# A new order of the work items in a two-layer transformer kernel: Q's and K's stacks apart, the cuts of the maxima further ahead of their transposes, the held residual behind the up matrices

## The chip, the cores and the metric

One core of one Trainium2 chip. The metric is the device time of one launch in microseconds (us). Before the change it was 1240.19 us, the median of 3 runs.

## What is computed

Eight batches of 512 tokens with 256 channels go through two layers. Layer 0 is a conditioned transformer block with a causal mask and an MLP, layer 1 an attention without mask between two conditioned normalizations. Cut to what matters:

```python
def layer0(x, condition):                    # x: (8, 512, 256) float32, condition: (8, 256)
    mod = silu(condition) @ Wada + bada      # (8, 1536)
    sh_a, sc_a, gt_a, sh_m, sc_m, gt_m = split(mod, 6, axis=1)
    xm = layernorm(x, g1, be1) * (1 + sc_a) + sh_a
    q, k, v = heads(xm @ Wqkv)               # 16 heads of 16 channels
    s = where(causal, q @ k.T / 4, -inf)
    x = x + gt_a * (merge(softmax(s) @ v) @ Wproj + bproj)
    xm = layernorm(x, g2, be2) * (1 + sc_m) + sh_m
    return x + gt_m * (gelu(xm @ W1 + b1) @ W2 + b2)      # W1: 256 -> 1024

def layer1(hidden, w):
    h = sln(hidden, w)                       # gamma(w) * layernorm + beta(w)
    q, k, v = heads(h @ Wqkv.T + bqkv)
    out = merge(softmax(q @ k.T) / 16 @ v) @ Wp.T + bp
    h1 = out + hidden
    return sln(h1, w) + h1
```

## The kernel before

**Order.** All the work is a sequence of items, written out by hand in three lists of tokens. HEAD is run once (for the passes -1, 0 and 1), RING once for each of the passes 2 to 6, TAIL once (7, 8 and 9); pass i has layer 0's batch i beside layer 1's batch i-1. `one_list` (L206) walks a list and calls the same function `work` for each engine, so TensorE (PE), VectorE (DVE), ScalarE (ACT), GpSimd (POOL) and the DMA queue of SyncE (SP) each get their own part of every item, all in the order of the list. An engine never overtakes within its own queue. Semaphore counts, banks and buffers follow from the order by counters (`ADDS`, L100 on).

**Items of attention.** There are 16 heads, 4 query tiles, and 16 steps (4 groups of heads by 4 key tiles) for each layer and batch.
- `s`, a scan: scores of one head and query tile, to find each row's maximum. PE makes them in a PSUM bank (L972, and L975 for the mask in layer 0), DVE takes the maximum (L759, 128, 256, 384 or 512 wide in layer 0, always 512 in layer 1). Scans share four banks with all dense items.
- `nm..`: POOL cuts the negated maxima of eight heads ("a" or "b"; of four heads with `_0` to `_3`) in three parts, four instructions (L575 to L581). `max..`: PE transposes them (L1117), ACT copies (L684) and its own queue moves them under the queries (L686). An attention step of those heads waits for that DMA.
- `a` and `p`: three heads, then the fourth, of one step: scores transposed on PE (L953) and the exponentials on ACT (L621). In layer 0 POOL masks the diagonal (L541).
- `o`: the products of two steps with V (L942). `t`: ACT copies a group's output to OE (L636).
- `pack` (SP, L439 and L441, five DMAs), `recip` (SP, L447 and L452, the reciprocals to DRAM and spread back), `scale` (DVE, L907), or `fold` and `merge` in the first and last batch: the division by the sums.

**Other items.** `stat` and `norm` (DVE, L768 and L808) normalize, `turn` (PE L1052, ACT L651) transposes and modulates, `q`, `k` (L1064) and `v` multiply; q and k are cut into three bf16 parts in PART by ACT (L666), DVE (L834 to L842) and POOL. `stackq` and `stackk` (SP, L416, 12 DMAs each in two halves of the heads) copy these parts into QS and KS, where the scans and scores read them:

```python
for part in range(3):
    wait(sp, (high_act, cut_low, cut_low)[part], ready[part])
    for r in range(CUTS):
        if parts[r] == part:
            sp.dma_start((QS, KS)[side][n][r:CUT_ROWS:CUTS, heads, :],
                         PART[rows, side, part, :, :]).then_inc(stack_dma[n][half], 16)
```

At `stackq` SP waits until ACT has done the exponentials of all scores ahead of it in the list, then issues Q's first half (6 DMAs); at `stackk` it issues K's first half, Q's second and K's second (18). A scan that begins a half of the heads waits on PE for that half of Q and K. `proj` (L1037 with WP, DVE L871 and L875) adds the attention to the residual. `up_0` to `up_7` (PE L1088, ACT L671 with Gelu, another table of ACT than that of Exp) and `down_0` to `down_3` (L1037 with W) are the MLP. `row0`, `row1`, `keep0` are SP's loads of the row vectors and the next batch (L461, L467, L474); with row0 goes an addition on POOL (L587). `hold1` is an addition on POOL (L596) of layer 1's bias to the residual that is kept for proj1. `gain1` and `close1` end layer 1. `mods` is 24 products of 128 x 128 weights with 8 columns, in pairs (48 matmuls, L918), which make the modulation; its first eight pairs are made before the lists. `rows` (PE L1017) turns the row vectors and, on SP, issues the loads of the later weights.

**Places.** In a pass, the items between k1 and turn_a hold most scans of layer 1, which are all 512 wide; behind turn_a come layer 0's q, k, v, projection and MLP.

Of the kernel before, what the change touches and what calls it, by code (L numbers as in the profile page):

```python
# [58 lines left out]
HEAD = """
    stat_a norm_a turn_a q0 stackq0 k0 stackk0 mods rows s v0 s s s s s s s s s s s s s s s s s s s s s s s s s  # L60
    s s s s s s s nm0_0 s s max0_0 s s s s s s s s a s s s s row0 s p a s nm0_1 s keep0 p s s s a s max0_1 p o a
    p a s o s nm0_2 s p a s s s p s s a stat_a t max0_2 s p s o a p a nm0_3 p o a t norm_a p a max0_3 p turn_a o
    fold0_0 a p a o t p a p fold0_1 a p o a p q0 o fold0_2 t fold0_3 merge0 proj0 stackq0 k0 norm_m v0 stackk0
    turn_m up_0 s up_1 s s s s up_2 s s up_3 s s s s s up_4 s s s s s up_5 s s s s s up_6 s s s s up_7 s s s s s
    s down_0 s nm0a down_1 max0a down_2 down_3 s a s s s p s a p norm_1 s s o s s s a s s row0 p turn_1 s a s s
    s s keep0 s s stat_a s p q1 k1 stackq1 s norm_a o v1 s a stackk1 s s t s p s a s s s s s p turn_a s a s s
    nm0b p max0b s s a s s s o s p s s a s s o s p s a s p s s s t a s o s p s a s p s a s s p s s o s s t a s p
    a s s s nm1a s p s o s a s p s max1a s o t pack0 s recip0 v0 s s a q0 p s a s s p scale0 s s s a stackq0 o p
    proj0 a s s norm_m p k0 a s s o p turn_m a s s s up_0 s t up_1 up_2 up_3 stackk0 s s p up_4 up_5 s a s s s o
    p s s nm1b hold1 s a s s p s s up_6 s s up_7 o s max1b down_0 a down_1 p down_2 s a s s t p down_3 a o s p s  # L70
    a s s p s s s a s p s s s s s a s s o s p s s t a s s norm_1 nm0a s s o p s turn_1 s a s s s max0a q1 p s k1
    s""".split()
# [8 lines left out]
TAIL = """
    stackq1 o t a s s s p s s pack1 a s p s a s s p stackk1 a s s o p s a s s recip1 s s o s s p s s s t s a s
    nm0b s row1 p a s p s s max0b s a s s o s s p s a s s o s s s p s a s p s a s s t s s p a o p s s a s s o t
    s s row0 s p s a s s p s nm1a scale1 s a o p s a max1a s p proj1 o s t a s v1 pack0 recip0 gain1 p s a s p a
    p s s a s o p scale0 s s o close1 proj0 a p s s norm_m s s a p a s hold1 turn_m s s s s up_0 s up_1 up_2
    up_3 up_4 s s up_5 up_6 s s up_7 s s down_0 s down_1 t down_2 s s p nm1b down_3 max1b a norm_1 o p o turn_1
    a q1 t k1 p a p stackq1 stackk1 a p a o s s p s s a s s s o s t s p s s a s p s s s a s nm1_0 p s s o row1 s
    max1_0 s s a s s s s s p o s s a s p s s a s s p v1 s t nm1_1 a s p s max1_1 s s a s o s pack1 s p s s a s p
    s recip1 o s a s s p s nm1_2 s a s p t s s max1_2 s s s a s s o s p s a s keep0 o t s p s s a p fold1_0
    nm1_3 a o p max1_3 scale1 a proj1 p gain1 a p o t a close1 p a p o row1 a p fold1_1 o fold1_2 hold1 t  # L90
    fold1_3 merge1 proj1 gain1 close1""".split()
# [1084 lines left out]
```

How the kernel before makes its waits and increments, by code:

```python
def wait(eng, sem, value):  # L150
    if value > 0:
        eng.wait_ge(sem, value)
# [239 lines left out]
        @block.sync  # L392
        def _(sp):
            sp.dma_start(CT[:], cond_t).then_inc(cond_load, 16)
            by_row = wada.rearrange("(k p) n -> p k n", p=P)
            sp.dma_start(WADA[:, :, 0:2 * D], by_row[:, :, 0:2 * D]).then_inc(ada_load, 16)
            sp.dma_start(XIN[:], x[0].rearrange("(t p) d -> p t d", p=P)).then_inc(x_dma, 16)
            sp.dma_start(WQKV[0][:], wqkv0.rearrange("(k p) n -> p k n", p=P)).then_inc(qkv_load[0], 16)
            sp.dma_start(WADA[:, :, 2 * D:6 * D], by_row[:, :, 2 * D:6 * D]).then_inc(mod_load, 16)
            sp.dma_start(WGB, wgb1.rearrange("(k p) n -> p k n", p=P)).then_inc(mod_load, 16)
            sp.wait_ge(ones_pool, 1)
            for n in range(2):
                sp.dma_start(KS[n][CUT_ROWS:ALL_ROWS, :, :], ONES).then_inc(ones_load, 16)
# [13 lines left out]
            def work(at, kind, what, b):  # L419
                if kind != "chunk":
                    return
                if what == "rows":
                    sp.wait_ge(set_dve, ROWS_READY)
                    sp.dma_start(rows_dram, ROWS.rearrange("p (r d) -> p r d", d=D)).then_inc(rows_out, 16)
                    sp.dma_start(WP[0][:], wproj0.rearrange("(k p) n -> p k n", p=P)).then_inc(proj_load[0], 16)
                    sp.dma_start(W1[:], w1.rearrange("(k p) n -> p k n", p=P)).then_inc(up_load, 16)
# [75 lines left out]
            run_passes(work)
            sp.wait_ge(store_dma, 16 * (B + 1))
```

## Time and profile before

| | |
|---|---|
| runs | 1240.56, 1240.19, 1234.33 us, median 1240.19 |
| profiled execution, its own time | 1239.17 us |
| its span | 1237.4 us |
| mean granted clock of PE | 0.986 |
| busy: PE, DVE, ACT, POOL | 94%, 69%, 55%, 23% |
| HID to down: PE, mean of one 128x256 matmul (L1037, W) | 380 ns |
| maximum, mean over all widths (L759) | 583 ns x1024 |
| exponential, mean over all widths (L621) | 524 ns x1024 |

Times in the profile are microseconds from the start of the span, unless ns is written. PE's matmuls overlap in their pipeline and their ends are modelled, so its busy share says less than the chain of work that ended last: that chain is followed back from the last instruction, at each step to what released it or to the instruction before it on its engine, and its shares say who set the end. The waits list an engine's idle time by what ended it.

### The profile page before, as it was taken

To read this page: it belongs to the slowest core of one execution; us is meant where nothing else is said; L and a number is where in the kernel's file an instruction comes from. 1 tells how busy PE (TensorE), PEld (TensorE's weight loads), DVE (VectorE), ACT (ScalarE), POOL (GpSimd) and SP (SyncE) were. 2 spreads that over 40 slices of the span, in tenths; PEclk is the share of its full clock that TensorE was granted. 3 is DMA by queue.
4 is the path that set the end of the run, shared out by engine and by line. 5 is a ranking of instruction groups with operands and counts; after the bars stand their busy time and mean duration, and the time that the engine had idled before them with its cause. 6 is when DMAs were issued, how large, how long until landed. Compare 5 with 4: busy or idle time off the path is not lost.

```text
span 1237.4 us, 18599 instructions
## 1 busy us (share of the span) xinstructions
PE 1164.9 (94%) x6604; PEld 591.7 (48%) x6604; DVE 849.1 (69%) x1779; ACT 676.6 (55%) x1346; POOL 279.7 (23%) x378
## 2 busy tenths in 40 slices
PE   7888999999999998999899999999989999999995
PEld 5434644464444644555345644546445553445332
DVE  4835498637886579836887379855888368764775
ACT  1173245656557465565656466565645656553673
POOL 1133032311432024301233013320233002310003
PEclk9799999999999999999999999999999999999999
DMA  4603031302432042500623024410425005200311
GB/s 166 206 2 103 3 124 33 107 14 72 111 93 65 18 113 71 139 2 18 164 44 115 2 80 104 105 54 18 118 66 139 1 2 148 55 17 32 86 33 43
DMA packets 59190, 89.35 MB, mean 72 GB/s; under 512 B 12914, under 2 KB 23762, under 8 KB 59098
## 3 DMA queue, kind: packets, MB, share of 16 engines
q1 hardware_dynamic: 58078, 87.35, 25.4%
q8 instruction: 53, 0.87, 0.3%
q10 hardware_dynamic: 1020, 0.81, 0.2%
q14 instruction: 39, 0.32, 0.1%
HBM read 24.41 MB, written 4.70 MB: 24 GB/s over the span
## 4 chain that ended last, share of the span: by engine, by line
PE 63%; DVE 19%; ACT 5%; SPq 5%; DMA 3%; issue 3%; POOL 1%; ACTq 0%; DVEq 0%; POOLq 0%
PE X L1037 15%; DVE MX L759 10%; PE OP L942 10%; PE X L1064 9%; PE X L1088 9%; PE SC L953 8%; PE X L972 8%; SPq L416 4%; ACT E L621 3%; DMA OC<-OE 2%; DVE STAT L768 2%; DVE XN L808 2%; DVE XR L875 1%; DVE TMP L871 1%; PE X L1052 1%
## 5 line engine op out<-in xcount | busy, mean ns | idle before, releaser
L759 DVE TENSOR_REDUCE MX<-X 128x1 f32<-128x512 f32 (+3 forms) x1024 | 533.2, 583 | 178.4 <-PE X L975 95.4
L621 ACT ACTIVATE E<-SC 128x512 f32<-128x512 f32 (+3 forms) x1024 | 459.0, 524 | 325.8 <-PE SC L953 258.6
L972 PE MATMUL X<-KS,QS 96*128 96x512 bf16 (+3 forms) x1024 | 296.5, 346 | 11.6 <-DVE MX L759 7.5
L953 PE MATMUL SC<-QS,KS 99*128 99x512 bf16 (+3 forms) x1024 | 276.1, 342 | 19.6 <-ACT E L621 12.6
L942 PE MATMUL OP<-E,V 128*32 128x512 f32 (+3 forms) x2048 | 208.2, 524 | 5.2 <-ACT OE L636 5.0
L953 PEld LDWEIGHTS SC<-QS,KS 99*128 99x128 bf16 x1024 | 93.7, 97 | 168.3 <-ACT E L621 105.9
L972 PEld LDWEIGHTS X<-KS,QS 96*128 96x128 bf16 x1024 | 97.4, 98 | 160.2 <-DVE MX L759 52.9
L541 POOL TENSOR_SCALAR_AFFINE_SELECT E<-E 128x512 f32<-128x512 f32 x128 | 87.0, 683 | 249.1 <-ACT E L621 249.1
L1088 PE MATMUL X<-XT,W 128*128 128x512 f32 x256 | 119.1, 598 | 1.2 <-ACT XT L651 1.2
L1064 PE MATMUL X<-XT,WQKV 128*128 128x512 f32 x256 | 118.2, 607 | 1.4 <-ACT XT L651 1.4
L1037 PE MATMUL X<-W,HID 128*128 128x256 f32 x512 | 115.3, 380 | 0.3 <-ACT HID L671 0.3
L975 PE MATMUL X<-CAUSAL,ID 128*128 128x128 bf16 x512 | 105.8, 223 | 0.0
L942 PEld LDWEIGHTS OP<-E,V 128*32 128x32 f32 x2048 | 53.9, 110 | 108.2 <-issue 79.3
L1037 PEld LDWEIGHTS X<-W,HID 128*128 128x128 f32 x512 | 96.3, 190 | 14.0 <-ACT HID L671 0.8
L555 POOL TENSOR_TENSOR RSTD<-VE,HALF 128x4 f32<-128x4 f32 x32 | 32.9, 1029 | 275.2 <-DVE VE L773 274.4
L671 ACT ACTIVATE HID<-X,VF 128x512 f32<-128x512 f32 x64 | 43.3, 687 | 58.7 <-PE X L1088 58.4
L1064 PEld LDWEIGHTS X<-XT,WQKV 128*128 128x128 f32 x256 | 48.7, 194 | 53.5 <-issue 49.3
L871 DVE TENSOR_TENSOR TMP<-X,ROW 128x512 f32<-128x512 f32 x32 | 22.0, 687 | 74.9 <-PE X L1037 74.9
L575 POOL TENSOR_SCALAR NMP<-MX 128x32 bf16<-128x32 f32 (+1 forms) x36 | 8.7, 242 | 281.6 <-DVE MX L759 256.8
L1088 PEld LDWEIGHTS X<-XT,W 128*128 128x128 f32 x256 | 46.4, 190 | 45.1 <-issue 41.5
L975 PEld LDWEIGHTS X<-CAUSAL,ID 128*128 128x128 bf16 x512 | 51.3, 100 | 22.7 <-issue 8.8
L1037 PE MATMUL X<-WP,OC 128*128 128x256 f32 x256 | 58.7, 382 | 1.6 <-issue 0.8
(92 smaller groups left out, 922.9 us busy)
## 6 DMA issues: line engine op xcount, KB each, us to landing
QS<-PART SPq DMA_DIRECT2D x192, 128.0 KB, 2.4
KS<-PART SPq DMA_DIRECT2D x192, 128.0 KB, 2.5
OC<-OE SPq DMA_DIRECT2D x56, 128.0 KB, 3.8
RB<-recip_sums SPq DMA_DIRECT2D x56, 128.0 KB, 2.6
XIN<-in_x SPq DMA_DIRECT2D x8, 512.0 KB, 4.9
ROW<-row_vectors SPq DMA_DIRECT2D x8, 512.0 KB, 3.7
out<-OUT SPq DMA_DIRECT2D x7, 512.0 KB, 3.2
W<-in_w SPq DMA_DIRECT2D x2, 1024.0 KB, 7.3
```

What stands on the lines that cost most here:

```text
L416: sp.dma_start((QS, KS)[side][n][r:CUT_ROWS:CUTS, heads, :], PART[rows, side, part, :, :]).then_inc(stack_dma[n][half], 16)
L541: g.affine_select(out=block, in_=block, compare_op=ALU.is_ge, fill=zero, base=0, pattern=[[0, 4], [1, P]], channel_multiplier=-1)\
L621: a.activation(E[:, at["tick"].index() % 3, j, lo:T], SC[(at["head"].index() + j) % 3][:, lo:T], ACT.Exp, scale=HD ** -0.5 if layer == 0 e ...
L671: a.activation(HID[:, ht, :], bank(0)[:], ACT.Gelu, bias=B1[:, ht:ht + 1])\
L759: v.reduce_max(MX[:, qt, h:h + 1], X[at["bank"].index() % BANKS][:, 0:w], AX.X, negate=True)\
L942: ins = t_.matmul(OP[32 * j:32 * j + 32, lo:T], V[layer][:, kt, h * VW:h * VW + 32], E[:, (at["step"].index() + n) % 3, j, lo:T], start=kt ...
L953: t_.matmul(SC[(at["head"].index() + j) % 3][:, lo:T], KS[stacks(layer, b)][0:ALL_ROWS, h, kt * P:kt * P + P], QS[stacks(layer, b)][0:ALL_ ...
L972: ins = t_.matmul(bank[:, 0:w], QS[stacks(layer, b)][0:CUT_ROWS, h, qt * P:qt * P + P], KS[stacks(layer, b)][0:CUT_ROWS, h, 0:w], start=Tr ...
L975: ins = t_.matmul(bank[:, qt * P:w], ID16[:], CAUSAL[:], start=False, stop=True)
L1037: ins = t_.matmul(psum[:, t % 2 * D:t % 2 * D + D], rows[:, kt, t * P:t * P + P], weights(kt), start=kt == 0, stop=kt == depth - 1)
L1064: ins = t_.matmul(psum[:], WQKV[n][:, kt, lo:lo + P], XT[:, kt, :], start=kt == 0, stop=kt == KT - 1)
L1088: ins = t_.matmul(psum[:], W1[:, kt, ht * P:ht * P + P], XT[:, kt, :], start=kt == 0, stop=kt == KT - 1)
```

## The change

Only the three lists are changed. Each holds the same tokens as before, in another order; no instruction is added, removed or changed in shape. In the middle passes stackq0 moves from behind q0 to behind turn_m, away from k0, and hold1 from behind turn_m to behind up_7; nm1a moves ahead of v1 and apart from max1a, nm0b and max0b further apart, and pack1 ahead of stackk1. In HEAD, mods moves from behind the first stacks to ahead of the first turn_a, and the first q0 of batch 1 behind merge0. In TAIL the order of the first stretch stays about the same and the folds move. The scans and steps between are spread anew. The middle list and the first lines of HEAD:

```diff
@@ -57,38 +57,39 @@
 EARLY = 9
 HEAD = """
-    stat_a norm_a turn_a q0 stackq0 k0 stackk0 mods rows s v0 s s s s s s s s s s s s s s s s s s s s s s s s s
-    s s s s s s s nm0_0 s s max0_0 s s s s s s s s a s s s s row0 s p a s nm0_1 s keep0 p s s s a s max0_1 p o a
-    p a s o s nm0_2 s p a s s s p s s a stat_a t max0_2 s p s o a p a nm0_3 p o a t norm_a p a max0_3 p turn_a o
-    fold0_0 a p a o t p a p fold0_1 a p o a p q0 o fold0_2 t fold0_3 merge0 proj0 stackq0 k0 norm_m v0 stackk0
-    turn_m up_0 s up_1 s s s s up_2 s s up_3 s s s s s up_4 s s s s s up_5 s s s s s up_6 s s s s up_7 s s s s s
...
+    stat_a norm_a mods turn_a q0 stackq0 k0 stackk0 rows v0 s s s s s s s s s s s s s s s s s s s s nm0_0 s
+    s s max0_0 s s s s s s s s s nm0_1 a s s s s p s s a s p s s s a s p max0_1 s s s a row0 s keep0 s o
+    nm0_2 p a s s s p s s max0_2 o s s t a s s s s p s a p o a s s s p a o t s nm0_3 p a fold0_0 p max0_3 a
+    o p a p a fold0_1 p stat_a norm_a o t a p fold0_2 a p o a p o t turn_a fold0_3 merge0 q0 stackq0 proj0
+    k0 norm_m v0 turn_m up_0 up_1 up_2 stackk0 s s s s s s up_3 s s up_4 s s s s s s s s up_5 s s s s s s
+    up_6 s s up_7 s s s s s s s s nm0a down_0 down_1 max0a s down_2 s s s down_3 a s s s s p a p s s s a s
...
 RING = """
-    row0 s stackq1 a s p o a stackk1 s s t s s s p s s pack1 s a s o s s s p s s a s s s p s s a s s s p o s
-    nm0b s s recip1 a max0b s s s p s a s p s s t s a s o s s p s a s scale1 s p o row1 a s t s p proj1 a s s p
-    o s a p a p s s s o s t a keep0 s p s s s a s gain1 p o close1 a nm1a stat_a max1a s v1 p norm_a a o t s
-    pack0 p s turn_a s a s recip0 s s q0 p s s s a o stackq0 p s s a s scale0 k0 s s p proj0 a s s norm_m p v0 a
-    o s s p turn_m hold1 s s a s s t s p up_0 up_1 s o s a s s s up_2 s s up_3 stackk0 p s s nm1b up_4 up_5 s
-    up_6 max1b s o s s up_7 t s s a s s down_0 s p down_1 s a s s p down_2 down_3 a o s p s s a s s p s s s s a
-    s norm_1 s o s p s s s a s s s s s p turn_1 a s nm0a s s t max0a s p q1 a s s o p s k1 s""".split()
+    stackq1 o s t s s s a s row0 p s row1 s s s a s s pack1 s stackk1 p s s a s p s s a s s recip1 s o s s
+    s s p a s s s nm0b p s s keep0 o t a s s s p a s max0b s s p s s s o s a s s p a s s p o scale1 a s s s
+    p proj1 t o a s s s s p a p a s s p o t s s a s nm1a s p gain1 close1 stat_a v1 a max1a o s norm_a p a
+    p a s s p o t pack0 turn_a s a s s s recip0 q0 p s s s a o p s s s a s s scale0 p k0 s s a proj0 p v0
+    norm_m a o p s s turn_m s a stackq0 t s s s up_0 up_1 s s p s o s a s s s p s o t stackk0 s s s up_2
+    nm1b up_3 up_4 up_5 max1b s up_6 up_7 s s s a s s s hold1 down_0 down_1 p s s s a down_2 down_3 p s s a
+    o p s a s s s p s s s a s s p norm_1 o s s s s a s s s p t turn_1 s a o s s p s s a s nm0a s s s p q1
+    max0a s k1""".split()
 TAIL = """
-    stackq1 o t a s s s p s s pack1 a s p s a s s p stackk1 a s s o p s a s s recip1 s s o s s p s s s t s a s
-    nm0b s row1 p a s p s s max0b s a s s o s s p s a s s o s s s p s a s p s a s s t s s p a o p s s a s s o t
-    s s row0 s p s a s s p s nm1a scale1 s a o p s a max1a s p proj1 o s t a s v1 pack0 recip0 gain1 p s a s p a
...
+    stackq1 s a o t p s s a s row1 s p s s s o s s s s a s s s p s s pack1 a s s p a s stackk1 s s s s nm0b
+    p s o t s a s s s recip1 p a max0b s s p s o s a s s p s a s s p o s t a s p s s s a s s p o s s a s s
+    p a s s p o s t a s s p s nm1a s s row0 a scale1 s p o a s s p proj1 gain1 o t pack0 recip0 s max1a v1
+    a p s s s a p row1 s s s s a s s o s scale0 p a p s close1 proj0 a s s norm_m o p a p s s turn_m a s s
...
```

## Rows read from the trace of the kernel before

**Rows 1.** The page, part 4: the chain that ended last, by engine
```profile
PE 63%; DVE 19%; ACT 5%; SPq 5%; DMA 3%; issue 3%; POOL 1%; ACTq 0%; DVEq 0%; POOLq 0%
```

**Rows 2.** That chain in order of time: start, us, engine and operation
```profile
558.17 6.92 PE X L1037 x32
...
580.03 3.43 PE X L1064 x8
584.51 1.85 PE OP L942 x16
...
642.04 0.65 PE X L972 x3
```

**Rows 3.** Windows: stretch, length, busy PE, PEld, DVE, ACT, POOL, clock, DMA share, GB/s
```profile
733.62:783.70 50.08, 46.02 (x340) 22.19 (x339) 45.98 (x100) 29.30 (x76) 18.01 (x27) 1.00 0.41 111
783.70:877.00 93.30, 93.01 (x472) 49.09 (x471) 58.26 (x120) 55.99 (x93) 17.24 (x17) 1.00 0.20 54
```

**Rows 4.** Timeline of PE: start, length, line, output and inputs, count
```profile
730.93 3.65 PE L1064 MATMUL X<-XT,WQKV 128*128 128x512 f32 x8
```

**Rows 5.** Timeline of all engines around turn_a
```profile
782.32 1.37 DVE L808 TENSOR_SCALAR XN<-XIN,MV,RSTD 128x256 f32<-128x256 f32 x4
...
783.49 0.71 PE L1052 MATMUL X<-ID,XN 128*128 128x128 f32 x5
```

**Rows 6.** Lines by form, DVE, 702 to 845 us
```profile
L759 DVE TENSOR_REDUCE MX<-X 128x1 f32<-128x512 f32 x80 | 50.9, 682 | 9.5 <-PE X L972 7.6 <-PE X L975 1.9
```

**Rows 7.** Waits of PE, 558.2 to 702.3 us: us in total, times, longest
```profile
PE X L1117 <- POOL NMP L581: 1.8, 2, 1.2
PE OP L942 <- ACT OE L636: 1.3, 1, 1.3
```

**Rows 8.** The page, part 6: DMAs, count, KB each, us to landing
```profile
KS<-PART SPq DMA_DIRECT2D x192, 128.0 KB, 2.5
```

**Rows 9.** Timeline of SP in a middle pass
```profile
735.65 3.82 SPq L416 DMA_DIRECT2D KS<-PART  x6
...
747.33 0.60 SPq L439 DMA_DIRECT2D RS<-OE  x1
```

**Rows 10.** The chain in order of time: a DMA issued by pack1
```profile
750.50 3.88 DMA OC<-OE
```

**Rows 11.** Timeline of SP in the old kernel's last pass
```profile
1030.29 4.67 SPq L416 DMA_DIRECT2D KS<-PART  x6
...
1044.42 0.34 SPq L447 DMA_DIRECT2D recip_sums<-RR  x1
```

**Rows 12.** Timeline of PE, the start of that pass
```profile
1023.80 1.50 PE L942 MATMUL OP<-E,V 128*32 128x512 f32 x12
```

**Rows 13.** Lines: busy us, mean ns, idle before
```profile
L621 ACT ACT_TABLE_LOAD x20 | 25.7, 1283 | 4.9 <-PE OP L942 3.0 <-ACT NT L684 1.7
```

**Rows 14.** Timeline of PE in the head
```profile
10.65 2.21 PE L1052 MATMUL X<-ID,XN 128*128 128x128 f32 x8 [1.61 <-DVE XN L808]
13.81 9.95 PE L1064 MATMUL X<-XT,WQKV 128*128 128x512 f32 x16 [0.96 <-ACT XT L651]
...
27.75 3.56 PE L918 MATMUL SC<-CT,E 128*128 128x8 f32 x16
```

**Rows 15.** The tile E, landing of its first load
```profile
L401 SPq DMA_DIRECT2D E<-in_wgb x1: 695/695/695, 3.3 to 3.3; - x1
...
DMA to landing us min/median/max: 9.4/9.4/9.4
```

**Rows 16.** Timeline of SP in the head
```profile
24.88 4.73 SPq L416 DMA_DIRECT2D KS<-PART  x6
```

**Rows 17.** Windows of the head, columns as in rows 3
```profile
24.00:32.00 8.00, 7.31 (x45) 7.22 (x45) 3.66 (x9) 0.40 (x1) 0.00 (x0) 0.65 0.56 181
40.41:56.55 16.14, 13.92 (x83) 6.30 (x83) 16.14 (x42) 0.59 (x1) 3.19 (x5) 0.79 0.76 240
56.55:97.69 41.14, 35.23 (x279) 16.16 (x279) 18.51 (x46) 29.12 (x75) 15.62 (x31) 1.00 0.08 23
```

More of the change, by code:

```diff
@@ L65 @@
[L65 to L69, printed above, removed]
@@ L70 @@
-    p s s nm1b hold1 s a s s p s s up_6 s s up_7 o s max1b down_0 a down_1 p down_2 s a s s t p down_3 a o s p s
-    a s s p s s s a s p s s s s s a s s o s p s s t a s s norm_1 nm0a s s o p s turn_1 s a s s s max0a q1 p s k1
-    s""".split()
-RING = """
-    row0 s stackq1 a s p o a stackk1 s s t s s s p s s pack1 s a s o s s s p s s a s s s p s s a s s s p o s
-    nm0b s s recip1 a max0b s s s p s a s p s s t s a s o s s p s a s scale1 s p o row1 a s t s p proj1 a s s p
-    o s a p a p s s s o s t a keep0 s p s s s a s gain1 p o close1 a nm1a stat_a max1a s v1 p norm_a a o t s
-    pack0 p s turn_a s a s recip0 s s q0 p s s s a o stackq0 p s s a s scale0 k0 s s p proj0 a s s norm_m p v0 a
-    o s s p turn_m hold1 s s a s s t s p up_0 up_1 s o s a s s s up_2 s s up_3 stackk0 p s s nm1b up_4 up_5 s
-    up_6 max1b s o s s up_7 t s s a s s down_0 s p down_1 s a s s p down_2 down_3 a o s p s s a s s p s s s s a
-    s norm_1 s o s p s s s a s s s s s p turn_1 a s nm0a s s t max0a s p q1 a s s o p s k1 s""".split()
@@ L81 @@
-TAIL = """
-    stackq1 o t a s s s p s s pack1 a s p s a s s p stackk1 a s s o p s a s s recip1 s s o s s p s s s t s a s
-    nm0b s row1 p a s p s s max0b s a s s o s s p s a s s o s s s p s a s p s a s s t s s p a o p s s a s s o t
-    s s row0 s p s a s s p s nm1a scale1 s a o p s a max1a s p proj1 o s t a s v1 pack0 recip0 gain1 p s a s p a
[L85 to L91, printed above, removed]
+    stat_a norm_a mods turn_a q0 stackq0 k0 stackk0 rows v0 s s s s s s s s s s s s s s s s s s s s nm0_0 s
@@ new lines @@
+    s s row0 keep0 o norm_1 s s s turn_1 p s s s a p s s s s stat_a q1 a stackq1 norm_a s s k1 p o t v1 a s
+    s s p s a s s stackk1 p s s s o s s nm0b max0b a s s s turn_a p s s s a s s s p o t s s a s s s p a p s
+    s s a s o s p s a s s s p o t s a s s p s s s a o nm1a max1a s s s s p a p s s s s a s s p o t pack0
+    recip0 a s q0 p s s s a o p s a s p s s s scale0 s a o t p s proj0 k0 norm_m v0 turn_m s s a s s up_0
+    hold1 s s p up_1 up_2 up_3 up_4 s s s a up_5 up_6 stackq0 nm1b up_7 stackk0 s s s p o max1b a s s
@@ new lines @@
+    down_0 down_1 s p o t a down_2 p s s a s down_3 p o a s s s p s s a s p s s s s a norm_1 s o s t p s
+    turn_1 s s a s s s s s p o s s s a nm0a s s p s s s s a s s q1 p s k1 max0a""".split()
+RING = """
+    stackq1 o s t s s s a s row0 p s row1 s s s a s s pack1 s stackk1 p s s a s p s s a s s recip1 s o s s
[6 more added lines that the diff above has]
+    max0a s k1""".split()
@@ new lines @@
+TAIL = """
+    stackq1 s a o t p s s a s row1 s p s s s o s s s s a s s s p s s pack1 a s s p a s stackk1 s s s s nm0b
+    p s o t s a s s s recip1 p a max0b s s p s o s a s s p s a s s p o s t a s p s s s a s s p o s s a s s
+    p a s s p o s t a s s p s nm1a s s row0 a scale1 s p o a s s p proj1 gain1 o t pack0 recip0 s max1a v1
+    a p s s s a p row1 s s s s a s s o s scale0 p a p s close1 proj0 a s s norm_m o p a p s s turn_m a s s
+    s up_0 up_1 up_2 up_3 s s up_4 up_5 up_6 t up_7 s s s s hold1 down_0 down_1 down_2 down_3 p o a s p
+    keep0 s nm1b o norm_1 turn_1 max1b t q1 k1 a p a p stackq1 a stackk1 o p s s a s s s p s o t s s a s s
+    s p s a s s s p a s nm1_0 s p s s a s s o s max1_0 s p s s s s o t pack1 s s a s s s p v1 a s nm1_1 s p
+    s recip1 s s a max1_1 s p o s a s s s p s s a s s p o s s t a s s s p s nm1_2 s a max1_2 o p s s a s s
+    p s s s a s o t s p s s nm1_3 a p fold1_0 a max1_3 p o scale1 a p fold1_1 a p o a p t proj1 gain1
+    close1 a o p a fold1_2 p o t fold1_3 row1 merge1 hold1 proj1 gain1 close1""".split()
```

## The prediction

> **What bounds the kernel now.** I read the page first: TensorE (PE) counts as busy 94% of the span, but the chain of work that ended last gives PE 63%, VectorE (DVE) 19%, SyncE's DMA queue 5% [rows 1]. So part of the busy PE is a PE that starts late. The chain's own pieces give PE's pace: 3.46 us for the 16 matmuls of a down (half of the 6.92), 3.43 for a q or k, 1.85 for an attention product, 0.22 for a 512-wide scan or score [rows 2]. With the counts of one middle pass (128 scans, 128 scores, 16 products, 4 q and k, 4 v and proj, 8 up at half a q, 4 down, turns and maxima) these paces sum to 131.8 us, and a pass lasts 50.1 + 93.3 = 143.4 [rows 3]. About 11.6 us per pass are lost, 58 in the five middle passes. I call the PE time that the list puts ahead of an item, summed from the pass's start, its place.
>
> Where they are lost: those two stretches run from the end of k1 to the end of norm_a and on to the next k1. DVE is busy 46.0 of the first 50.1 us, and 58.3 of the other 93.3 [rows 3]. From k1 (place -3.5, start 730.93 [rows 4]) to turn_a (place 40.3, start 783.49 [rows 5]) PE's work is 43.8 us and the clock ran 52.6, so 8.8 of the 11.6 are lost there, behind DVE, which needs 682 ns for a 512-wide maximum [rows 6] of which PE makes the scores in 0.22 us. That is the bound which an order must shift. In the second stretch PE runs near its pace, and no order gains much.
>
> **The middle passes.** The lists hold the same items, so no instruction is added or taken away; only the order changes.
>
> (a) Maxima. PE waits for the last cut of the maxima by GpSimd (POOL) twice per pass, 1.8 us in all [rows 7]. New places: nm0b 11.6 and max0b 14.8 (was 12.1, 13.0), nm1a 31.8 and max1a 36.0 (was both 34.2), with v1 between. These waits go. But max1a stands in the DVE stretch: turn_a, the next item that needs DVE, started at 783.49, in the moment in which its rows came (the normalization runs 782.32 to 783.69 by parts) [rows 5]. A PE that arrives there sooner waits there. DVE's work up to norm_a stays the same but for one scan more ahead of norm_a and a fraction of one fewer ahead of k1: +0.4 us. What can come back is only that part of DVE's 4.1 idle us in this stretch (50.1 - 46.0) which other work now fills, some 1.4. Attend (0, layer 1) at place 38.5 needs max1a's copy and its DMA, some 3 us by the stacks' 2.5 to land [rows 8], behind place 36.0 + 0.4: 0.8 late at most, and only if DVE is not later still. I take nothing for it.
>
> (b) The sync queue. Six issues of the stacks take 3.8 us [rows 9]; now pack1 (5 issues) stands behind all 24, starts at 747.33 and its last DMA lands at 754.38 [rows 9, 10]. For the first group's output PE also waits 1.3 us [rows 7]. The new order is stackq1, row0, row1, pack1, stackk1, recip1: pack1 comes 9 us sooner and this wait goes. But K's first half, for which scan (1,0,0) waits, comes behind pack1. The last pass of the old kernel already has that order: there stackk1's first half is issued 1030.29 to 1034.96, 2.5 more to land, and recip1 starts at 1044.42 [rows 8, 11], 13.7 and 20.6 us after the pass began (1023.8 [rows 12]). With row0 and row1 ahead, but an earlier output copy: 13.6. The new scan (1,0,0) has place 10.1, and PE is 2.3 late there: 12.4. So PE and DVE wait 1.2 (bounds 0 and 2). The spread of the reciprocals lands near 27.6 (recip1 at 20.6, two DMAs behind each other, 2.5 each, and their issue), DVE reaches scale1 at about 26.8: 0.8 (0 to 1.5). Per pass DVE's idle time thus falls by 1.4 and rises by 2.0, with +0.4 of work: +1.0 at norm_a. PE's last 512-wide scans ahead of q0 then stand behind turn_a with free banks, which gives back some 0.8. I take +0.2 per pass (bounds -3.0 and +2.2), +1 for five passes.
>
> (c) Stacks apart in the second stretch. stackq0 goes from place 49.4 to 68.3, stackk0 stays (80.1, now 78.9). Begun at 68.3 + 9 us of lateness, 12 issues at 0.64 and a landing of 2.5 end 10.2 later, at place 78.5 against 78.9 of the first scan. Nothing, at worst 1.
>
> (d) hold1 goes from behind turn_m to behind up_7. It is one POOL instruction, and POOL is busy 17.2 of 93.3 us in this stretch [rows 3]. Nothing; if it lay ahead of a cut of the maxima it would cost its length, but nm1b stands before it now.
>
> (e) The up matrices stand closer (up_3 to up_5, up_6 with up_7), so ScalarE (ACT) switches its table less often, 1.28 us each [rows 13]. ACT is busy 56.0 of 93.3 us there [rows 3] and its exponentials are not last. Nothing, at best -0.5 per pass.
>
> **The head.** "mods" (24 pairs, 48 instructions) moves ahead of turn_a. Now turn_a starts at 10.65, q0 and k0 run to 23.76, and mods follows it to 31.31; 16 of its kind take 3.56 us [rows 14]. Its last operand is issued at 3.3 and lands 9.4 later, at 12.7 [rows 15], so turn_a no longer starts at 10.65: mods' 48 at 0.222 us are 10.7, begun at 12.7, and turn_a starts at 23.4, q0 and the stacks 12.7 us later. What is taken out behind (7.7 us) is hidden by rows, v0 and the stacks: K's first half is issued 24.88 to 29.61 [rows 16], so with 12.7 more and 2.5 to land it is there at 44.8, and the first scans wait for it. DVE's unbroken row of maxima, now from 40.41 [rows 17], starts near 44.7: +4.3 (3 to 6). Given back: 32 scans instead of 43 stand ahead of the first attention step, and DVE, busy 16.14 of 16.14 us with 42 of them [rows 17], takes 0.4 each: -4.4. From there to merge0 the stage lasts 41.1 us with ACT busy 29.1 [rows 17]; q0 leaves it for behind merge0 (-1.2), where its matmuls cover merge0's copies. Against it: the later weights now load during the first steps, so the row vectors land later too, and the masks on POOL stand behind row0: 0 to 3, say 2.6. Sum at proj0: +1.5 (-2 to +6). Behind it, turn_1 three places closer to down_3 and nm1a next to max1a (+1 each), less queueing behind down_3 (-1.5): +0.5.
>
> The clock in this stage: PE's granted clock was 0.65 from 24 to 32 us, while mods ran [rows 17], so it went down to the lower of the two levels (1.2 GHz) at some point there; 8-column matmuls did not hold it up. The Trainium skill ("TensorE: Matmul & The Clock Gate", What's actually happening) says that sustained activity keeps the clock at 2.4 GHz and idleness lets it fall, and this row does not agree if mods counts as activity. By the rule read plainly, mods ahead of q0 would warm PE up; that is rival D.
>
> **The tail.** Its first stretch has (b)'s order already: 0. Proj0 one place sooner (-0.5), the last steps spread over proj1 and the folds, against row1 ahead of pack1: 0. I take -0.5 (-3 to +2).
>
> **Sum.** +1 + 1.5 + 0.5 - 0.5 = +2.5 on the profiled execution's 1239.2 (1237.4 span and 1.8 around it): 1241.7, say 1242. The median of the runs shown is 1240.2 and the lowest 1234.3, so the profiled one is a fair middle.
>
> **Rivals.** A, faster: the waits of (a) and (b) are true losses, since the denser scans fill DVE's 4.1 idle us: 1.8 + 1.3 = 3.1 per pass [rows 7], 15.5 in five; with the head's +2 and the tail's -0.5, 1225. For it: they are among the longest gaps of a pass. Against: DVE's 46.0 of 50.1.
> B, slower: the sync queue. If K's first half and the reciprocals come late by their full amounts (1.2 and 0.8) and nothing is given back before the next norm_a, +2.2 per pass, 11, and the head +3: 1253. It decides from the point where stackk1's first half lands after PE reaches scan (1,0,0), 12.4 us into the pass. For it: the last pass's rows [rows 11]. Against: there DVE still had work.
> C, slower: in the head nothing is given back, because weights, maxima and row vectors share the DMA engines (busy 0.76 there [rows 17]): +4.3 and +3 instead of +2, with the middle passes' and the tail's +0.5: 1247.
> D: mods on PE ahead of q0 raises the clock, so that q0 and k0 (16 matmuls) take 2 x 3.43 = 6.9 us instead of 9.95 [rows 2, 14]: -3.1, 1239. The clock row above is against it.
>
> **How the numbers follow.** My forecast 0.46 (own range 1235 to 1247), A 0.28, B 0.17, C 0.06, D 0.03. 0.5% is 6.2 us, about what a measurement of this kernel can tell from no change: faster 0.30 (A, and the low end of mine), slower 0.24 (B, C and a little of mine), same 0.46. The range 1224 to 1253 takes in A and B to their middles and a little more.
>
> **What would show it.** Middle passes of 143 to 144 us; DVE busy over 45 us from k1 to norm_a, with idle time before the maximum of scan (1,0,0); no PE wait for POOL's cuts; pack1 issued within 6 us of stackq1; turn_a in the head at 23 us and the first unbroken maxima at 44 to 45. I am wrong if a pass takes 140 (A) or 146 (B), or if the first attention step comes after 60 us (C).

## The result and the profile after

The changed kernel takes 1246.07 us (median of 6 runs, 1244.15 to 1251.08) against 1239.89 for the kernel before in the same comparison: ratio 1.0066, 95% interval 1.0036 to 1.0095. The ratio compares the means of the runs and makes 8 us (4 to 12); the medians differ by 6.2. It is slower by more than my 2.5, inside the range. The profiled execution has a span of 1243.4 us.

The page's chain, by engine, answers [rows 1]:

```profile
PE 78%; DMA 6%; ACT 5%; SPq 4%; DVE 4%; issue 2%; POOL 0%; ACTq 0%; DVEq 0%; POOLq 0%
```

VectorE (DVE) is nearly gone from it (19% to 4%), and the kernel is no faster. The DMA share goes from 3% to 6%, and the rest of the chain is PE's own. Which DMAs PE now waits for is shown by the waits of TensorE (PE) over the whole run (us in total, times, longest one). The kernel before:

```profile
PE X L1117 <- POOL NMP L581: 8.8, 10, 1.2
...
PE OP L942 <- ACT OE L636: 5.0, 5, 1.5
...
PE SC L953 <- DMA QS<-NT: 1.2, 3, 0.6
```

The changed kernel (its lines are one higher from the lists on):

```profile
PE SC L954 <- DMA QS<-NT: 16.8, 9, 3.4
PE SC L954 <- ACT E L622: 8.5, 24, 0.6
PE X L973 <- DMA KS<-PART: 6.7, 6, 2.2
```

The waits for POOL's cuts and for the output copy are gone, 13.8 us together. New are 15.6 us more in attention steps that wait for the DMA of the maxima (QS<-NT, 16.8 against 1.2) and 6.7 in scans that wait for K's stack (KS<-PART). In one middle pass of the changed kernel (572.56 to 717.61 us), against [rows 7]:

```profile
PE SC L954 <- DMA QS<-NT: 1.7, 1, 1.7
PE X L973 <- DMA KS<-PART: 1.0, 1, 1.0
```

At four such waits PE's granted clock goes down. Columns as in [rows 3], four stretches of the changed kernel (the third last number is the clock):

```profile
308.00:320.00 12.00, 9.14 (x54) 4.74 (x47) 8.29 (x18) 5.35 (x13) 3.63 (x3) 0.72 0.77 195
356.00:364.00 8.00, 6.21 (x38) 3.50 (x39) 5.64 (x16) 5.10 (x13) 2.20 (x3) 0.79 0.17 51
500.00:512.00 12.00, 9.91 (x46) 4.87 (x45) 8.00 (x22) 7.02 (x15) 2.20 (x3) 0.72 0.32 68
648.00:656.00 8.00, 6.48 (x38) 3.11 (x39) 5.57 (x13) 4.81 (x10) 2.01 (x3) 0.79 0.07 20
```

At the lower level (0.5 of full speed), 28% of 12 us or 21% of 8 us are 3.4 or 1.7 us of PE's pace. These four take 10.2 us of PE's pace together, and at most that much time, since PE is idle in a part of them. The kernel before has one fall between 300 and 1000 us, at 900 to 904 (1.7 us). It is not a matter of this one execution: the mean granted clock over the whole kernel was 0.973 to 0.979 in the six runs of the changed kernel, and 0.982 to 0.992 in the 70 runs of the kernel before that the experiments below were compared with. A thousandth of it is 1.2 us of PE's pace. Where the time comes from, by the start of down_3 of each batch:

| down_3 of batch | 0 | 1 | 2 | 3 | 4 | 5 | 6 | 7 |
|---|---|---|---|---|---|---|---|---|
| before, us | 148.3 | 273.3 | 417.9 | 561.5 | 705.6 | 848.9 | 994.8 | 1122.7 |
| after, us | 153.3 | 277.0 | 426.2 | 572.6 | 717.6 | 860.5 | 1004.1 | 1128.4 |
| difference | 5.0 | 3.7 | 8.4 | 11.1 | 12.0 | 11.6 | 9.3 | 5.7 |

The head costs 4 to 5 us, the first two middle passes 7.4 (with three of the four falls), the other three give back 1.8, and behind the last down_3 of the middle list the difference falls from 9.3 to the 6.0 of the two spans: the tail gives back 3.3.

In the head, mods did what the sum said. PE's timeline (start, length, with the idle time before in brackets) answers [rows 14]:

```profile
12.57 7.00 PE L919 MATMUL SC<-CS,HID 128*128 128x8 f32 x32 [3.61 <-DMA E<-in_wgb]
19.42 3.56 PE L919 MATMUL SC<-CT,E 128*128 128x8 f32 x16
22.84 1.95 PE L1053 MATMUL X<-ID,XN 128*128 128x128 f32 x8
25.74 10.06 PE L1065 MATMUL X<-XT,WQKV 128*128 128x512 f32 x16 [0.96 <-ACT XT L652]
42.75 0.23 PE L973 MATMUL X<-KS,QS 96*128 96x128 bf16 x1 [2.17 <-DMA KS<-PART]
...
58.27 1.46 PE L954 MATMUL SC<-QS,KS 99*128 99x512 bf16 x3 [3.43 <-DMA QS<-NT]
```

Turn_a starts at 22.84 (forecast 23.4), q0 and k0 take 10.06 us, as long as before (9.95), and the first step of attention starts at 58.27, with a wait of 3.4 us for its maxima. The same 16 matmuls, cut at 31.5 us, and below them the first of mods in the kernel before:

```profile
25.74 6.20 PE L1065 MATMUL X<-XT,WQKV 128*128 128x512 f32 x7 [0.96 <-ACT XT L652]
31.00 4.81 PE L1065 MATMUL X<-XT,WQKV 128*128 128x512 f32 x10
```

```profile
23.60 2.85 PE L918 MATMUL SC<-CS,HID 128*128 128x8 f32 x25
```

The first seven start 0.85 us apart or more, the other nine 0.43, so PE's clock was at its lower level until some 31.7 us and at its full level behind that. Mods' own matmuls start 0.21 us apart here (48 in 10.3 us) and 0.11 apart in the kernel before, until its clock fell at 26.4 us: all of mods ran at the lower level here, and the clock did not rise behind it before q0 had run for 6 us. (A window of this trace that ends before 31.7 us shows a clock of 1.00 all the same, since the clock's record begins only there.)

### The profile page after: what moved, and what is told of

Its sections match the earlier page's. It is cut to its first block, busy times and chain, and to the rows that moved or that the text cites. A ratio compares the mean times of both kernels' runs of the same rounds, so it can differ in the third digit from the quotient of the medians.

```text
span 1243.4 us, 18589 instructions
## 1 busy us (share of the span) xinstructions
PE 1169.4 (94%) x6604; PEld 601.9 (48%) x6604; DVE 852.2 (69%) x1779; ACT 663.8 (53%) x1336; POOL 277.2 (22%) x378
## 4 chain that ended last, share of the span: by engine, by line
PE 78%; DMA 6%; ACT 5%; SPq 4%; DVE 4%; issue 2%; POOL 0%; ACTq 0%; DVEq 0%; POOLq 0%
PE X L1038 17%; PE OP L943 13%; PE SC L954 12%; PE X L973 12%; PE X L1089 9%; PE X L1065 9%; ACT E L622 4%; DMA QS<-NT 3%; PE X L1053 2%; SPq L442 2%; SPq L417 2%; PE X L976 1%; DMA KS<-PART 1%; DVE MX L760 1%; PE SC L919 1%
## 5 line engine op out<-in xcount | busy, mean ns | idle before, releaser
L954 PE MATMUL SC<-QS,KS 99*128 99x512 bf16 (+3 forms) x1024 | 278.8, 347 | 29.8 <-DMA QS<-NT 16.8
L973 PE MATMUL X<-KS,QS 96*128 96x512 bf16 (+3 forms) x1024 | 285.7, 345 | 15.5 <-DMA KS<-PART 6.7
L576 POOL TENSOR_SCALAR NMP<-MX 128x32 bf16<-128x32 f32 (+1 forms) x36 | 7.9, 220 | 277.0 <-DVE MX L760 189.0
```

The lines of the kernel that those rows point to most:

```text
L954: t_.matmul(SC[(at["head"].index() + j) % 3][:, lo:T], KS[stacks(layer, b)][0:ALL_ROWS, h, kt * P:kt * P + P], QS[stacks(layer, b)][0:ALL_ ...
L973: ins = t_.matmul(bank[:, 0:w], QS[stacks(layer, b)][0:CUT_ROWS, h, qt * P:qt * P + P], KS[stacks(layer, b)][0:CUT_ROWS, h, 0:w], start=Tr ...
```

## The experiments

Ratios are to the kernel before, run in the same comparison (its medians there: 1238.5, 1238.1 and 1238.8 us), with 95% intervals. One thousandth is 1.24 us.

### Which list costs what

The kernel before with one of its three lists exchanged for the changed one.

```diff
 new_head
-HEAD = """ ... before ... """
+HEAD = """ ... changed ... """
 new_ring
-RING = """ ... before ... """
+RING = """ ... changed ... """
 new_tail
-TAIL = """ ... before ... """
+TAIL = """ ... changed ... """
```

> The kernel before with only the first list (HEAD) replaced by the changed one. Theory M (the changed kernel loses its time where an attention step waits for the DMA of the maxima, and where PE's clock falls just behind such a wait): the two traces differ by 4.6 us of lost PE time at down_3 of batch 1, so 1239.9 + 4.6 = 1244.5, and with the wait of 2.9 us at the first attention step behind the list 1246 to 1248. Rival H (my forecast's head: +2.0): 1242. Rival C (nothing is given back behind mods): +7.3, 1247 with the first attention step of batch 0 no sooner than 58.

> The kernel before with only the middle list (RING) replaced. Theory M: attend (0, layer 1) waits some 1.8 us for the DMA of max1a in each of the five passes, and the clock falls behind some of these waits (3 us each, two of five in the trace of the changed kernel): the traces differ by 5.3 us between down_3 of batch 1 and of batch 6, so 1245. Rival S (the sync queue, K's first half late at scan (1,0,0) by 1.2 us, forecast +0.2 per pass): 1241. Rival A (waits for POOL's cuts truly saved): 1225 to 1230.

> The kernel before with only the last list (TAIL) replaced. Theory M and my forecast agree on a gain, but not on its size: the traces differ by -4.0 us of lost PE time from down_3 of batch 6 to the end: 1236. My forecast had -0.5: 1239.4. If the gain in the trace of the changed kernel was only the catching up of lateness from before the list, this kernel shows 1239 to 1240 as well.

Measured: new_head 1248.55 us, ratio 1.0077 (1.0048 to 1.0106); new_ring 1241.62, 1.0024 (0.9999 to 1.0048); new_tail 1233.9, 0.9956 (0.9936 to 0.9975). That is +9.5, +3.0 and -5.5 us, +7.0 together, against +8.2 (1.0066) for the three at once. The new head alone costs as much as the whole change (their intervals overlap), the middle list is hardly told from no change (near rival S's 1241, with theory M's 1245 inside the interval), and the tail is a gain of its own, so lateness that was caught up is not its reason. The head's time fits theory M and rival C alike, and its first attention step comes at 57.53 us, near C's 58; the next two sections part them. Behind its first 10 us, new_head's longest wait of PE is at the first attention step of batch 2:

```profile
312.19 1.26 PE L953 MATMUL SC<-QS,KS 99*128 99x512 bf16 x3 [3.87 <-DMA QS<-NT]
```

In the new head max0a is the last token (the old one has it ahead of q1), and the middle list, old or new, begins with steps that need its DMA.

### The end of the head

```diff
-... nm0a s s p s s s s a s s q1 p s k1 max0a
+... nm0a s s p s s s s a s s max0a q1 p s k1
```

> The changed kernel with one token moved in HEAD: max0a from the list's last place to ahead of q1, so that its DMA starts some 7.5 us of PE time sooner. Theory W (the new head's largest loss is the first attention step of batch 2, which waits 3 to 4 us for that DMA, and the clock falls behind the wait for another 1.7 to 3.4): 1246.1 - 3 - 2.5 = 1240.5, range 1239 to 1243. Rival H (that wait only takes up lateness that VectorE would cause anyway at norm_a of batch 3): 1246 to 1247, with the wait gone and the start of turn_a of batch 3 still at 361.

Measured: 1240.78 us, ratio 1.0021 (1.0002 to 1.0040). One token is worth 4.5 thousandths, 5.6 us (1 to 10), as theory W had it. In the profiled execution the first middle pass is 3 us shorter than in the changed kernel (146.2 against 149.2), and neither the wait of 2.9 us at 312 nor the fall there is left. Lateness of VectorE, the rival, would have left the time as it was.

### mods

```diff
-    stat_a norm_a mods turn_a q0 stackq0 k0 stackk0 rows v0 ...
+    stat_a norm_a turn_a q0 stackq0 k0 stackk0 mods rows v0 ...
```

> The changed kernel with mods moved back behind the first stacks. By the steps of my forecast mods costs +4.3 at the first unbroken maxima (44.7 against 40.4) and the 32 instead of 43 scans give it back only if they stand there: without mods ahead, turn_a starts at 10.6, the first attention step at 56 - 4.4 - ... = 51 to 52 instead of 58, and the kernel takes 1246.1 - 4.3 - 2 (less waiting for the first maxima) = 1240 to 1242. Rival L (the first attention steps then wait for rows and for the row vectors, whose place in the load queue stays): 1245 to 1246. Rival K (PE's clock, which stood at its lower level from 27 to 38 us before and not in the changed kernel, falls there again): 1243 to 1244.

Measured: 1237.33 us, ratio 0.9984 (0.9966 to 1.0002): 8.2 thousandths or 10 us less than the changed kernel. More than expected (the interval of the difference is some 4 us to either side). PE's timeline, turn_a and the first attention step, and then DVE's first unbroken maxima, here and in the changed kernel:

```profile
10.36 2.20 PE L1053 MATMUL X<-ID,XN 128*128 128x128 f32 x8 [1.41 <-DVE XN L809]
...
51.81 1.45 PE L954 MATMUL SC<-QS,KS 99*128 99x512 bf16 x3 [2.38 <-DMA QS<-NT]
```

```profile
37.66 12.85 DVE L760 TENSOR_REDUCE MX<-X 128x1 f32<-128x128 f32 x32
```

```profile
43.07 12.87 DVE L760 TENSOR_REDUCE MX<-X 128x1 f32<-128x128 f32 x32 [0.81 <-PE X L976]
```

The unbroken maxima start 5.4 us sooner than in the changed kernel, the first attention step 6.5 (51.81 against 58.27), and proj0 of batch 0 6.8: 94.1 against 100.9. That is the price of mods in front, 6.5 to 6.8 us, within the interval of the 10. Behind the head nothing else changed: the profiled passes have the same lengths as in the changed kernel (148.9, 146.1, 145.0, 142.8, 143.4 us against 149.2, 146.4, 145.0, 142.9, 143.6), and down_3 of batch 6 starts 7.5 us sooner. The clock does fall again from 28.0 to 34.8 us, as rival K said, and the kernel is faster all the same. Mods ran at the full level here (48 matmuls in 5.3 us). The forecast's split of the head was off: mods cost 5.4 at the maxima and 6.5 at the attention, and not 4.3.

### Both at once

```diff
-    stat_a norm_a mods turn_a q0 stackq0 k0 stackk0 rows v0 ...
-... a s s q1 p s k1 max0a
+    stat_a norm_a turn_a q0 stackq0 k0 stackk0 mods rows v0 ...
+... a s s max0a q1 p s k1
```

> The changed kernel with both tokens of HEAD put right: mods behind the first stacks and max0a ahead of q1. Theory W (the two prices are separate): 1246 - 8.7 - 5.3 = 1232, range 1230 to 1235, faster than the kernel before by 0.5%. Rival O (both only shift where the falls of the clock come, and overlap): 1236 to 1238.

Measured: 1231.89 us, ratio 0.9945 (0.9919 to 0.9970). The two prices add up (1.0066 - 0.0082 - 0.0045 = 0.9939), and the rest of the change is a gain of 7 us (4 to 10) against the kernel before. The new tail alone gave 5.5 of that, so little of it is left for the middle list and the rest of the head.

### The wait for the maxima in the middle passes

In the changed kernel the way of max1a is, on ScalarE and its queue, around the wait of PE in the fourth of the windows above (layer 1's batch 3):

```profile
645.28 0.57 ACT L685 ACTIVATE NT<-X 24x512 bf16<-24x512 bf16 x1
645.88 0.73 ACTq L687 DMA_DIRECT2D QS<-NT  x1
```

```profile
649.52 1.46 PE L954 MATMUL SC<-QS,KS 99*128 99x512 bf16 x3 [1.74 <-DMA QS<-NT]
```

Copy, issue and landing take 4.2 us (645.28 to 649.52), where I had put some 3. Two kernels take the wait away in two ways.

```diff
 max_early, in RING
-nm1a s p gain1 close1 stat_a v1 a max1a o s norm_a
+nm1a s p gain1 close1 stat_a max1a v1 a o s norm_a
 attend_late, in RING
-norm_a p a p a s s p o t pack0 turn_a
+norm_a p a p s s o t a p pack0 turn_a
```

> The changed kernel with one token moved in RING: max1a from behind v1 and one attention step to ahead of v1. Theory M: max1a's DMA starts 3.5 + 0.7 us sooner, attend (0, layer 1) no longer waits for it (1.8 us per pass now), PE waits for POOL's cut up to 1 us instead, the falls of the clock at 360, 504 and 652 us go: -0.8 to -1.8 per pass and -3 for each fall: 1246.1 - 9 = 1237, range 1234 to 1241. Rival DVE (what PE wins there it waits for at turn_a, since VectorE bounds the stretch): 1246, with the wait moved to turn_a.

> The changed kernel with layer 1's first attention step in RING put behind two scans and the product (14, 15), which stood behind it. Theory P (the wait for max1a's DMA is a delay that other work can cover; VectorE doesn't bound the stretch): the wait falls from 1.8 to 0.6 us or less, -1.1 per pass and one or two falls of the clock fewer: 1246.1 - 5.5 - 2 = 1239. Rival V (VectorE bounds the stretch, so turn_a starts when norm_a is done): turn_a starts as before and the kernel takes 1245 to 1246.

Measured: max_early 1247.45 us, ratio 1.0070 (1.0044 to 1.0096), no gain; attend_late 1241.57, 1.0018 (0.9990 to 1.0047), 6 us less than the changed kernel (1 to 11). Where the wait of max_early went, in its waits of PE and its timeline:

```profile
PE X L1117 <- POOL NMP L581: 11.6, 5, 2.3
```

```profile
644.10 0.39 PE L1117 MATMUL X<-ID,NMP 128*24 128x128 bf16 x4 [2.32 <-POOL NMP L581]
```

PE now waits 2.3 us per pass for POOL's cut (1.7 for the DMA in the changed kernel), one step earlier in the same chain (last maximum, cut, transpose, copy, DMA, attention step). Theory M had at most 1 us there, and the rival had it at turn_a. A transpose that comes sooner doesn't shorten the chain, whose start is the last maximum of the half. The falls did not go either: its profile has three between 300 and 1000 us (312, 500 and 933). With attend_late other work lies over the wait. In one of its passes PE's timeline shows what is left of it:

```profile
786.73 0.39 PE L972 MATMUL X<-KS,QS 96*128 96x512 bf16 x1 [0.64 <-DVE V L856]
787.39 0.39 PE L972 MATMUL X<-KS,QS 96*128 96x512 bf16 x1 [0.27 <-DVE V L856]
787.76 1.01 PE L942 MATMUL OP<-E,V 128*32 128x256 f32 x16
788.71 0.82 PE L953 MATMUL SC<-QS,KS 99*128 99x512 bf16 x3
789.98 0.39 PE L953 MATMUL SC<-QS,KS 99*128 99x512 bf16 x1 [0.45 <-ACT E L621]
```

The wait for the DMA is gone and 0.9 us for banks that DVE empties has come. Its second to fourth pass, without a fall, last 143.5 to 143.8 us, and those of new_ring 142.9 to 143.5. So the pass itself is no shorter, and theory P's 1.1 us per pass did not come back. Turn_a starts 57.6 to 57.9 us behind the start of q1 in these passes, and 57.4 and 58.0 in the changed kernel's last two, as rival V said of its start: V is not refuted for this list. The gain of 6 us goes with falls of the clock that are missing: its only fall between 300 and 1000 us is at 932 to 940, and its mean clock over six runs is 0.983 against the changed kernel's 0.977. One of the falls that are missing, at 312 us, lies ahead of any wait that this edit touches.

### The falls of the clock

To tell the wait from the fall behind it, this kernel keeps the waits and gives PE work in them. The condition takes in layer 1's first step of seven batches, the five middle passes and one on either side.

```diff
+if s == 0 and (layer == 1 and b < B - 1 or layer == 0 and b == 2):
+    wait(pe, exp_done, at["head"].at(1, -2))
+    for _ in range(8):
+        t_.matmul(SC[at["head"].index() % 3][:], KS[layer][0:CUT_ROWS, 0, 0:P],
+                  QS[layer][0:CUT_ROWS, 0, :], start=True, stop=True)
 if s % (TT if grouped(layer, b) else STEPS // 2) == 0:
     wait(pe, max_dma[layer], 16 * maxima_before(layer, b, s))
```

> The changed kernel with 8 more matmuls of 0.22 us each (their output is never read) ahead of PE's wait for the DMA of max1a in the middle passes and of max0a at batch 2, 1.76 us of work in each of those waits of 1.7 to 2.9 us. Theory C (behind these waits the granted clock falls, because PE stood idle, and that is part of the price): no fall at 312, 360, 504 and 652 us, 1.7 to 3.4 us each less: 1246 - 5 = 1241. Rival D (the waits are the whole price; the falls come wherever they come): 1246 to 1248, with as many falls as before.

Measured: 1242.12 us, ratio 1.0032 (1.0015 to 1.0048), 4 us less than the changed kernel with 14 us of matmuls more. The interval of this difference, 0 to 8 us, just reaches nothing; the clock says more. The windows that had the falls:

```profile
308.00:320.00 12.00, 10.62 (x68) 4.59 (x67) 9.60 (x18) 6.08 (x12) 2.99 (x2) 1.00 0.78 199
356.00:364.00 8.00, 7.63 (x59) 3.62 (x52) 7.00 (x22) 5.20 (x13) 2.20 (x3) 1.00 0.21 71
500.00:512.00 12.00, 11.64 (x64) 5.60 (x64) 9.56 (x26) 7.75 (x18) 2.19 (x3) 1.00 0.45 90
648.00:656.00 8.00, 8.00 (x47) 3.93 (x46) 5.78 (x11) 6.12 (x12) 0.00 (x0) 1.00 0.46 62
```

The clock stays at its full level (1.00 in all four, 0.72 to 0.79 in the changed kernel). One execution could be luck: between 300 and 1000 us four other kernels with the same middle list and no filling have four, two, two and one fall (mods_back, max0a_early, mods_max0a, new_ring), and the two with it have none (this one and the next below). The mean clock over all runs agrees: 0.985 here against 0.977 in the changed kernel. So it was PE's idle time that let it fall there. The Trainium skill ("TensorE: Matmul & The Clock Gate", What's actually happening) says that idleness lets the clock fall, and these rows agree. A fall doesn't follow every wait: in the changed kernel the steps at 794 and 938 us wait as long and keep 1.00. Nor does each stand at a long wait: the kernel before falls at 900 us, where no wait of PE reaches 1.5 us, and this kernel still has falls in the head, at 1044 us and behind, 23 us of PE's pace in its whole profile against 26 in the changed kernel's.

The same eight matmuls, in the kernel with both tokens of the head put right, at the first attention step of all and in the middle passes:

```diff
+if s == 0 and (layer == 1 and 1 <= b < B - 1 or layer == 0 and b == 0):
+    ... the same eight matmuls
```

> The same kernel with 8 unread matmuls (1.76 us) ahead of PE's wait for the DMA of the maxima at the first attention step of batch 0 and at layer 1's first step in each middle pass. Theory C (PE idle before the fall): the falls behind these waits go, two or three of 1.7 to 3.4 us: 1232 - 4 = 1228. If the other kernel shows few falls there, 1231 to 1232.

Measured: 1230.43 us, ratio 0.9924 (0.9899 to 0.9948), the fastest of all; against the kernel without them (0.9945) the intervals overlap, so that difference is not shown. The mean clock rose from 0.982 to 0.986, and its profile has no fall between 160 and 1200 us.

### Does VectorE bound the stretch from k1 to turn_a?

```diff
-v.reduce_max(MX[:, qt, h:h + 1], X[at["bank"].index() % BANKS][:, 0:w], AX.X, negate=True)
+v.reduce_max(MX[:, qt, h:h + 1], X[at["bank"].index() % BANKS][:, 0:w - P * layer], AX.X, negate=True)
```

> The kernel before with layer 1's maxima taken over 384 of the 512 columns (that part of the computation is changed: the row maximum leaves out the last 128 scores). DVE takes 0.13 us less for each of 64 scans of a pass, some 50 of them between k1 and turn_a: 6.5 us less of DVE's 46.0 there. Theory V (VectorE bounds that stretch): k1 to turn_a falls from 52.6 towards 46, a pass from 143.4 to 137 or 138, the kernel to 1240 - 35 - a bit in the lists around = 1200 to 1210. Rival P (the chain maximum, cut, transpose, DMA bounds it by its delays): at most 1 us per pass, 1233 or more.

Measured: 1232.61 us, ratio 0.9965 (0.9947 to 0.9983): 4 us, not 35. The windows from k1 to turn_a, the kernel before and this one:

```profile
730.93:783.49 52.56, 48.50 (x346) 23.23 (x345) 47.33 (x103) 30.67 (x78) 18.01 (x27) 1.00 0.40 108
```

```profile
726.16:778.44 52.28, 48.08 (x345) 23.28 (x344) 44.02 (x104) 30.65 (x78) 17.40 (x27) 1.00 0.38 109
```

DVE is busy 3.3 us less (not the 6.5 expected: 33 of layer 1's maxima lie in the stretch and not 50) and the stretch is 0.3 us shorter. In the other four middle passes it is 0.05 to 0.6 us shorter. DVE had 90% of the stretch before, and still did not set its length. Of the 8.8 us between 52.6 and my sum of 43.8, PE is idle for 4.1 in the old order, 3.8 of it in named waits (POOL's cuts 1.8, exponentials 1.1, output copy 0.5, banks 0.4). The other 4.7 lie inside its 48.5 busy us, which are more than the paces that I had summed.

### The sync queue

```diff
 pack_late, in RING
-... pack1 s stackk1 p s s a ... recip1
+... stackk1 pack1 s p s s a ... recip1
```

> The changed kernel with the sync queue's old order in RING: stackk1 ahead of pack1. By my forecast K's first half then lands some 4 us sooner, the wait of 1.0 to 1.3 us at scan (1,0,0) goes, and PE waits 1.3 for the output copy as in the kernel before: +-0.3 per pass, 1245 to 1247. Rival S (K's wait was the only true loss of the two): 1246.1 - 5 = 1241. Rival O (the output copy's wait is the greater): 1248.

Measured: 1271.33 us, ratio 1.0264 (1.0233 to 1.0294), 25 us slower than the changed kernel, and none of the expectations had it. SP's, DVE's and PE's timelines in one pass, and PE's waits for banks in the whole run:

```profile
618.59 0.59 SPq L439 DMA_DIRECT2D RS<-OE  x1
```

```profile
620.83 0.55 DVE L903 RECIPROCAL RR<-RS 128x64 f32<-128x64 f32 x1 [5.96 <-DMA RS<-OE]
```

```profile
621.67 0.59 PE L972 MATMUL X<-KS,QS 96*128 96x512 bf16 x1 [5.37 <-DVE MX L759]
```

```profile
PE X L972 <- DVE MX L759: 26.2, 24, 5.4
```

With pack1 behind the 24 issues of the stacks, its DMA of the sums comes 6 us after DVE has reached recip1 in its own order. DVE waits with the maxima of the scans queued behind the reciprocal, the four banks are full, and PE waits 5.4 us. That comes in four of the five middle passes (4.3 to 5.4 us), and makes 21 us more than the 5.3 of the changed kernel's waits for banks; the clock falls at each of the four, and its mean is 0.970 against 0.977. In the changed kernel pack1 is issued first:

```profile
603.97 0.60 SPq L440 DMA_DIRECT2D RS<-OE  x1
...
608.14 4.91 SPq L417 DMA_DIRECT2D KS<-PART  x6
```

and recip1 makes DVE wait once in the whole run, for 2.2 us. So pack1 ahead of stackk1 is what lets recip1 stand as early in the list as it does; the kernel before had recip1 behind nm0b, and could have the stacks first.

## Why the prediction came out as it did

The direction was right and the size was not: +8 against +2.5, just beyond the bound of 0.5% on the slower side, where I had a chance of 0.24. Step by step:

- *What bounds the stretch behind k1.* Wrong for the old list. I took DVE's 46.0 of 50.1 us [rows 3] and the place of turn_a right behind norm_a [rows 5] for proof that DVE sets the pace. With 3.3 us less of DVE's work there, the stretch was 0.3 shorter. The stretch is PE's own work, larger than my sum of paces by 4.7 us, and a few chains of delay.
- *(a) Maxima.* That the waits for POOL's cuts go was right. "I take nothing" for attend (0, layer 1) was the wrong step of the middle passes: it waits 1.7 to 1.9 us in each of the five. I had its delay at 3 us, with the landing of another DMA in place of its own; it was 4.2. With the wait comes a fall of the clock in three of five passes of the profiled execution, a term that I did not have.
- *(b) The sync queue.* The sum was right to a tenth: K's first half was to be there 13.6 us into the pass; the last of its DMAs landed 13.5 us after it in the pass that began at 455.0 us, and scan (1,0,0) waited 0.8 us there, 1.0 in the next pass, 0.3 and 1.1 in the two behind (forecast 1.2). That the order of pack1 and stackk1 matters for DVE's place at recip1 as well I had seen only as a gain of one wait of 1.3 us; the old order costs 5 per pass.
- *Passes.* Without falls a changed pass lasts 142.9 to 143.5 us (new_ring) against 143.3 to 144.1 before: -0.5, where I had +0.2. Still the list alone came out at +3 us (interval 0 to 6). Its profiled execution is one of the quick ones (span 1234.8) and shows one fall in its five passes; the clocks of the other executions show where the rest goes. Over its 12 runs the mean clock is 0.982, against 0.987 of the kernel before, some 6 us of PE's pace, and the time follows the clock from run to run: 1233.96 us at 0.988, 1247.49 at 0.975. My sign of being wrong, a pass of 146 us, was met in two of the five passes of the changed kernel, by the waits for the maxima and the falls; B's queue had 0.8 us in one of the two.
- *(c), (d), (e).* In the middle passes no wait for the stacks of layer 0, none for hold1; the ten table loads less show in ScalarE's instructions (1336 against 1346) and nowhere in the time.
- *The head.* Turn_a at 22.84 (forecast 23.4) and proj0 +1.3 (forecast +1.5) were right in the profile, the second by luck. The first unbroken maxima came 2.7 us later than before (43.07 against 40.41) and not 4.3. From there to the first attention step ten scans fewer gave back 0.9 us and not 4.4, since that step then waited 3.4 for its own maxima; and the steps behind took 0.4 less, where I had 1.4 more. The pair of profiles also hides the price of mods: 6.5 us, measured by moving mods alone. The term that I did not have is max0a as the last token of HEAD. My sum has turn_1 and nm1a behind proj0 and not the distance from max0a to the next pass's first step. It cost 5.6 us. The whole head was to cost 2.0 and cost 9.5 in new_head.
- *The tail.* -0.5 was too little; it is -5.5 (0.9936 to 0.9975). Why is open: over the whole run PE's waits for exponentials went from 12.6 to 8.5 us, but behind the last down_3 of the middle list they are 2.7 before and 2.4 in the changed kernel, so they are not the reason; no run took the tail apart.
- *Rivals.* A's premise (true losses) held for the waits, and its time didn't, since other waits of the same size came. B's mechanism, at the point that I named, is real, and its price was 1 us per pass or less; the other order cost 25 us by another way, DVE's place at recip1. C has the right place, the head, and the right size; little was given back there indeed, but for the wait for the first maxima and for max0a, and no run shows that shared DMA engines had a part. D is out: q0 and k0 took 10.06 us, with the clock at its lower level through mods and the first seven of their matmuls.

## What to carry over

For each item moved, look at both ends of its chain: what it waits for, and who waits for its DMA, past the end of the list too. A wait removed by distance on one side was made again on the other here, and cost more where PE's clock fell with it. A high busy share of an engine, even 90% with its result just in time, is no proof that it bounds; shorten its work and look at the stretch. When two orders trade waits, try the change list by list and token by token: two tokens cost 15 us here, and the rest of the change was a gain of 7, most of it the tail's.
